# Six-layer local-attention network: scaling on POOL, values through a copy by DMA, feed-forward once per 512 tokens

## What is computed

```python
# DIM 128, DEPTH 6, HEADS 16, DIM_HEAD 64, WINDOW 32, DIM_INNER 341
def attn_layer(x, Wqkv, qs, ksc, Wo):
    q, k, v = jnp.split(x @ Wqkv, 3, -1)            # each 16 heads of 64
    q = l2norm(q) * qs
    k = l2norm(k) * ksc
    q = q * cos * scale + rotate_half(q) * sin * scale
    k = k * cos * inv + rotate_half(k) * sin * inv
    out = local_attention(q, k, v)                  # each query sees itself and 32 keys back
    return out @ Wo
def ffn_layer(x, g, bln, W1, b1, W2, b2):
    xn = (x - mu) / jnp.sqrt(var + 1e-05) * g + bln
    a, gate = jnp.split(xn @ W1 + b1, 2, -1)
    return a * jax.nn.gelu(gate, approximate=False) @ W2 + b2
for i in range(DEPTH):
    x = attn_layer(shift_tokens(x), ...) + x        # shift_tokens moves half of the width by one token
    x = ffn_layer(shift_tokens(x), ...) + x
```

## Time and profile before

| | us |
|---|---|
| median of three runs (5686.42 to 5718.4) | 5706.67 |
| the profiled execution | 5696.51 |
| its span, from the first to the last instruction | 5694.7 |
| busy over the span: PE, DVE, ACT, POOL | 4468.9, 3603.6, 2963.1, 1958.8 |
| the stage of the change: first `mix_out` to the last | 2104.7 to 4858.2 |

### The profile page before, as it was taken

The page is one execution under the profiler, slowest core; times in us unless marked ns, Lnnn a source line. Parts: engine busy times, 40 slices in busy tenths (PEclk is TensorE's granted clock), DMA queues, the critical chain, the costliest instruction groups (busy, mean ns, idle before and its releaser), DMA issues. The chain is left out here.

```text
span 5694.7 us, 89214 instructions
## 1 busy us (share of the span) xinstructions
PE 4468.9 (78%) x28284; PEld 3096.7 (54%) x28284; DVE 3603.6 (63%) x7261; ACT 2963.1 (52%) x8154; POOL 1958.8 (34%) x1203
## 2 busy tenths in 40 slices
PE   6887987888644458888888888888888888588788
PEld 4655665555411136666666666666666666355566
DVE  5554224455578867777777777777777777344422
ACT  3333434443233336666666666666666666233433
POOL 3433003232045444444444444444444434122300
PEclk8888999999755579999999999999999999566799
DMA  0000000000000010000000000000000000000000
GB/s 18 1 2 35 0 0 20 1 1 14 3 0 0 0 50 1 0 0 22 0 0 22 0 0 22 0 0 22 0 0 0 0 0 1 17 1 0 0 30 7
DMA packets 26280, 41.43 MB, mean 7 GB/s; under 512 B 12112, under 2 KB 18664, under 8 KB 25448
## 3 DMA queue, kind: packets, MB, share of 16 engines
q1 hardware_dynamic: 26088, 39.04, 2.0%
HBM read 36.93 MB, written 2.10 MB: 7 GB/s over the span
## 5 line engine op out<-in xcount | busy, mean ns | idle before, releaser
L1426 PE MATMUL ps<-l2f_wqkv,l2f_xsT 128*128 (+3 forms) x1536 | 741.4, 605 | 97.1 <-DVE xnT L1621 90.3
L1358 POOL TENSOR_TENSOR l2f_rn<-l2f_ss,neghalf 128x16 f32<-128x16 f32 x192 | 564.7, 2941 | 436.1 <-DVE l2f_ss L1615 436.1
L1803 ACT ACTIVATE l2f_p<-ps,l2f_negmax 128x96 f32<-128x96 f32 x1536 | 501.7, 338 | 282.7 <-DVE l2f_negmax L1646 279.1
L1364 POOL TENSOR_TENSOR l2f_cosd<-xnT,l2f_rot 128x1024 f32<-128x1024 f32 x192 | 487.2, 2542 | 174.8 <-DVE xnT L1621 174.8
L1484 PE MATMUL ps<-l2f_pT,l2f_vw 96*128 96x128 f32 x3072 | 423.1, 281 | 40.4 <-DVE l2f_pT L1668 40.4
L1426 PEld LDWEIGHTS ps<-l2f_wqkv,l2f_xsT 128*128 128x128 f32 (+1 forms) x1536 | 243.4, 178 | 347.8 <-issue 197.4
L1818 ACT COPY l2f_oT<-ps 64x256 f32<-64x256 f32 x768 | 281.3, 366 | 269.8 <-PE ps L1484 258.3
L1484 PEld LDWEIGHTS ps<-l2f_pT,l2f_vw 96*128 96x128 f32 x3072 | 381.7, 195 | 61.4 <-issue 56.5
L1384 POOL TENSOR_TENSOR l2f_rstd<-l2f_mv,neghalf 128x1 f32<-128x1 f32 x96 | 52.8, 550 | 1051.5 <-DVE l2f_mv L1680 1051.5
L1457 PEld LDWEIGHTS ps<-l2f_kT,l2f_qz 128*128 128x128 f32 x3072 | 399.2, 194 | 1.4 <-issue 0.3
L1457 PE MATMUL ps<-l2f_kT,l2f_qz 128*128 128x96 f32 x3072 | 398.7, 273 | 0.0
(11 more groups left out here) (354 smaller groups left out, 10607.0 us busy)
## 6 DMA issues: line engine op xcount, KB each, us to landing
l2f_wqkv<-L_ffn_Wqkv_dram SPq DMA_DIRECT2D x18, 512.0 KB
l0f_w<-L_w_dram SPq DMA_DIRECT2D x2, 2304.0 KB
l3f_w<-L_w_dram SPq DMA_DIRECT2D x2, 2048.0 KB
l2f_wo<-L_ffn_Wo_dram SPq DMA_DIRECT2D x6, 512.0 KB
l2f_w<-L_ffn_W_dram SPq DMA_DIRECT2D x6, 341.0 KB
l2f_b<-L_ffn_b_dram SPq DMA_DIRECT2D x6, 341.0 KB
l1f_w<-L_w_dram SPq DMA_DIRECT2D x1, 1152.0 KB
k_turn<-l3a_kF SPq DMA_DIRECT2D x4, 256.0 KB, 2.0
```

Source lines behind the costliest of these rows:

```text
L1358: nc.gpsimd.tensor_tensor(rn[:, k], ss[:, k], g.neghalf[:, 0:HEADS], ALU.pow).then_inc(rn_ready, 1)
L1364: nc.gpsimd.tensor_tensor(cosd[:, k].rearrange("p (h d) -> p h d", d=DH), nrm[:, k].rearrange("p (h d) -> p h d", d=DH), rot[:, k, 0, t].u ...
L1426: ins = nc.tensor.matmul(g.ps[0:rows, 2 * (k % 2) + hf], x, wqkv[:, bass.ds(weight_slot(it), 1), c0 + hf * 512:c0 + (hf + 1) * 512] .rearr ...
L1803: ins = nc.scalar.activation(p[:, n % 2, c], g.ps[:, 4, c * KW:(c + 1) * KW], ACT.Exp, bias=negmax[:, col:col + 1], accum_out=rowsum[:, co ...
```

## The change

- **Scaling**: `scale` moves from DVE to POOL. DVE keeps the reciprocal (`inverse_sums`), and POOL's slot takes the four products between its other work.
- **Values**: they are projected once for 128 tokens (k = 2 only, in banks 0 and 1), copied by ACT into `vt`, and moved by two or three DMAs of SP into the two windows of `vw`. `copy_values` stands ahead of the last `exps`. `turn_qk(ahead, 0)` moves on PE ahead of `turn(now, 3)`, and `copy_q` on ACT ahead of `copy_outputs(now, 2)`.
- **Feed-forward**: it runs once in an iteration, one iteration late (`fed`), in the slots t = 1 (three matmuls of 128 x 512 for the gates, their copies, one GELU over 128 x 1536), t = 2 (three matmuls for the other half, product on DVE with the bias) and t = 3 (twelve matmuls with W2, `feed_out` over 512 tokens). Hidden units lie on partitions, so the transposes and their copies go. POOL copies W1 and its biases (`fix_weights`) once in an iteration.
- The loop of the program has two iterations in its body; at the end three slots of feed-forward alone are added. SP loads the first layer's weights after `band_ready`, and the next ones behind the values of a layer's first iteration.

The diff, cut to the queues and the new functions:

```diff
+            final = Iteration(ITERATIONS - 1, 1)
+            for stages in slots(final, last=True):
                 slot(*stages)
-            slot(NONE, NONE, (ITERATIONS - 1, TILES - 1))
+            slot(NONE, NONE, (final, TILES - 1), NONE)
+            for t in range(1, TILES):
+                slot(NONE, NONE, NONE, (final, t))
...
+            def move_values(it, t):
+                w = QBS * (t % 2)
+                sp.wait_ge(v_copied, at(it, TILES, t + 1))
+                sp.wait_ge(pv_done, at(it, STEPS2, PER * (t - 1)))
+                if t:
+                    sp.dma_start(vw[0:WINDOW, w], vt[P - WINDOW:P, (t - 1) % 2]).then_inc(v_moved[t % 2], 16)
+                sp.dma_start(vw[WINDOW:KW, w], vt[0:QB, t % 2]).then_inc(v_moved[t % 2], 16)
+                sp.dma_start(vw[:, w + 1], vt[P - KW:P, t % 2]).then_inc(v_moved[t % 2], 16)
+            sp.wait_ge(band_ready, 1)
+            load_weights(0)
+            for it in range(ITERATIONS):
+                for t in range(TILES):
+                    move_values(it, t)
+                if it % BATCH == 0 and it // BATCH + 1 < DEPTH:
+                    load_weights(it // BATCH + 1)
...
+            def scale(it, t, i):
+                if t is None:
+                    return
+                n = PER * t + i
+                if t == 3 and i == 3:
+                    pool.wait_ge(hT_ready, at(it, 3, -3))
+                pool.wait_ge(rinv_ready, at(it, STEPS2, n + 1))
+                nc.gpsimd.tensor_tensor(
+                    p[:, n % 2], p[:, n % 2],
+                    rinv[:, QUAD * n:QUAD * (n + 1)].unsqueeze(2).broadcast_to([P, QUAD, KW]), ALU.mult).then_inc(scaled, 1)
+            def fix_weights(it, t):
+                if t == 3:
+                    nc.gpsimd.tensor_copy(w1c[:, it.odd], w1[:, bass.ds(weight_slot(it), 1)]
+                                          .rearrange("p a c -> p (a c)")).then_inc(w1_ready, 1)
+            def slot(ahead, now, behind, fed):
                 inverse_deviation(*behind)
+                scale(*now, 0)
                 inverse_norms(*ahead, 0)
+                scale(*now, 1)
+                inverse_norms(*ahead, 1)
                 scaled_rotary(*ahead)
-                inverse_norms(*ahead, 1)
                 cosines(*ahead, 0)
+                scale(*now, 2)
                 cosines(*ahead, 1)
+                scale(*now, 3)
+                fix_weights(*now)
...
-                if k < 2:
-                    x, rows, c0 = xsT[:, WINDOW + t * P:WINDOW + (t + 1) * P], P, k * HD
-                else:
-                    w = QBS * t + k - 2
-                    x, rows, c0 = xsT[:, w * QB:w * QB + KW], KW, 2 * HD
+                    pe.wait_ge(nrm_ready, at(it, 2 * TILES, 2 * t + 1))
+                x, c0 = xsT[:, WINDOW + t * P:WINDOW + (t + 1) * P], k * HD
...
+            def hidden(f, t, c):
+                if t not in (1, 2):
+                    return
+                pe.wait_ge(w1_ready, at(f, 1, 1))
+                pe.wait_ge(xnT2_ready, turned_behind(f, t))
+                if t == 2 and not c:
+                    pe.wait_ge(hg_ready, at(f, 3, 3))
+                if c:
+                    pe.wait_ge((hg_ready, hT_ready)[t - 1], at(f, 3, c))
+                r0, rows = CH[c]
+                c0 = (DI, 0)[t - 1] + r0
+                nc.tensor.matmul(g.ps[0:rows, 7], w1c[:, f.odd, c0:c0 + rows], xnT2[:, f.odd],
                                  start=True, stop=True).then_inc(hid_ready, 1)
...
+            def feed(f, t):
+                if t != 3:
+                    return
+                pe.wait_ge(xnT2_ready, turned_behind(f, t))
+                pe.wait_ge(hT_ready, at(f, 3, 3))
+                for n in range(TILES):
+                    for c, (r0, rows) in enumerate(CH):
+                        ins = nc.tensor.matmul(g.ps[:, 7, n * P:(n + 1) * P], hT[0:rows, c, n * P:(n + 1) * P],
+                                               w2[0:rows, bass.ds(weight_slot(f), 1), c].rearrange("p a c -> p (a c)"),
+                                               start=(c == 0), stop=(c == 2))
                 ins.then_inc(ff_ready, 1)
-            def slot(ahead, now, behind):
+            def slot(ahead, now, behind, fed):
                 mix(*behind)
                 turn_y(*ahead)
                 scores(*now, 0)
@@ -1559,19 +1635,18 @@
                 scores(*now, 2)
                 turn(*now, 1)
                 pv(*now, 0)
-                hidden(*behind, 1)
+                hidden(*fed, 0)
                 scores(*now, 3)
                 project(*ahead, 2)
                 turn(*now, 2)
                 pv(*now, 1)
-                hidden(*behind, 0)
-                project(*ahead, 3)
+                hidden(*fed, 1)
+                turn_qk(*ahead, 0)
                 turn(*now, 3)
                 pv(*now, 2)
-                turn_hidden(*behind)
-                turn_qk(*ahead, 0)
+                hidden(*fed, 2)
+                feed(*fed)
                 pv(*now, 3)
-                feed(*behind)
                 turn_qk(*ahead, 1)
...
-            def scale(it, t, i):
+            def inverse_sums(it, t, i):
                 if t is None:
                     return
                 n = PER * t + i
                 dve.wait_ge(probs_ready, at(it, STEPS2, n + 1))
                 nc.vector.reciprocal(rinv[:, QUAD * n:QUAD * (n + 1)],
                                      rowsum[:, QUAD * n:QUAD * (n + 1)]).then_inc(rinv_ready, 1)
-                dve.wait_ge(rinv_ready, at(it, STEPS2, n + 1))
-                nc.vector.tensor_tensor(
-                    p[:, n % 2], p[:, n % 2],
-                    rinv[:, QUAD * n:QUAD * (n + 1)].unsqueeze(2).broadcast_to([P, QUAD, KW]), ALU.mult).then_inc(scaled, 1)
...
+            def gate_hidden(f, t, c):
+                if t != 2:
+                    return
+                rows = CH[c][1]
+                dve.wait_ge(hid_ready, at(f, 6, 4 + c))
+                dve.wait_ge(gelu_ready, at(f, 1, 1))
+                dve.wait_ge(ff_ready, at(f, 1, 0))
+                nc.vector.scalar_tensor_tensor(hT[0:rows, c], g.ps[0:rows, 7], w1c[0:rows, f.odd, HB + c:HB + c + 1],
+                                               hg[0:rows, c], ALU.add, ALU.mult).then_inc(hT_ready, 1)
+            def feed_out(f, t):
+                if t != 3:
+                    return
+                dve.wait_ge(ff_ready, at(f, 1, 1))
+                nc.vector.tensor_tensor(yt[:], g.ps[:, 7].rearrange("p (t d) -> p t d", d=D), ym[:, f.odd],
+                                        ALU.add).then_inc(yt_ready, 1)
+                dve.wait_ge(yt_ready, at(f, 1, 1))
+                nc.vector.tensor_tensor(g.gate[:, bass.ds((f & (BATCH - 1)) * TILES, TILES), :], yt[:],
+                                        b2[:, bass.ds(weight_slot(f), 1), :].broadcast_to([P, TILES, D]),
                                         ALU.add).then_inc(y_ready, 1)
...
-            def slot(ahead, now, behind):
+                nc.vector.tensor_tensor(ym[:, it.odd, t], yb[:, t], g.ps[:, 6, 0:D], ALU.add).then_inc(y_mixed, 1)
+            def slot(ahead, now, behind, fed):
                 fetch(*ahead)
                 mix_out(*behind)
                 maxima(*now, 0)
                 affine_of(*behind)
                 moments_of(ch, *behind)
-                scale(*now, 0)
+                inverse_sums(*now, 0)
                 normalize_shifted(*behind)
                 maxima(*now, 1)
                 norms(ch, *ahead, 0)
                 copy_probs(*now, 0)
-                scale(*now, 1)
+                inverse_sums(*now, 1)
                 maxima(*now, 2)
                 norms(ch, *ahead, 1)
                 copy_probs(*now, 1)
                 normalize(*ahead, 0)
-                scale(*now, 2)
+                inverse_sums(*now, 2)
                 maxima(*now, 3)
-                bias_hidden(*behind, 1)
                 swap(ch, *ahead, 0)
                 normalize(*ahead, 1)
-                scale(*now, 3)
+                inverse_sums(*now, 3)
                 copy_probs(*now, 2)
-                bias_hidden(*behind, 0)
+                gate_hidden(*fed, 0)
                 rotate(ch, *ahead, 0)
-                gate_hidden(*behind)
+                gate_hidden(*fed, 1)
                 swap(ch, *ahead, 1)
                 copy_probs(*now, 3)
+                gate_hidden(*fed, 2)
+                feed_out(*fed)
                 rotate(ch, *ahead, 1)
-                feed_out(*behind)
...
-            def copy_values(it, t, j):
+            def copy_values(it, t):
                 if t is not None:
-                    act.wait_ge(projected, at(it, 4 * TILES, 4 * t + j + 3))
-                    nc.scalar.copy(vw[:, (QBS * t + j) % (2 * QBS)], banks(2 * j, 2)[0:KW]).then_inc(v_copied, 1)
+                    act.wait_ge(projected, at(it, 3 * TILES, 3 * t + 3))
+                    for u in (t - 2, t - 1):
```

(33 more changed lines are left out.)

158 lines of the change are left out of this document (67 added, 91 removed).

## The result

The changed kernel takes **6439.23 us** (median of 4 runs, 6422.83 to 6443.82) against 5705.01 of the kernel before (4 runs beside it). The ratio is 1.128, with an interval from 1.125 to 1.132. The prediction said 6140, with a range from 5850 to 6370: the sign is right, but the loss is 734 us where 443 were expected, and the time lies outside the range.

A forecast was written before the change was run, and what follows sets the result against it. It took a slot to be bound by a chain of handovers between engines, no single engine being full. 5696.5 + 343 (slots) + 15 (start and end) + 86 (clock falls) = 6140 us, range 5850 to 6370.

The forecast's parts named there:

- The second turn: PE's second turn of p in a slot: 2.5 us later, since POOL's second scaling stands behind a power of 2.91 us.
- The price of a scaling: One scaling product on POOL: 0.83 us taken, up to 1.4 with a wait for the port behind one DVE product.
- The fourth maxima: DVE's fourth maxima in a slot: moved from 3045.45 to about 3047.95 by the later second turn, with no slack.
- The copy of the values: Values' part on PE and ACT: saved projection (1.9 us of PE) and second copy lie off the path, DMAs mostly hidden.
- The three copies behind `copy_q`: ACT's third `copy_outputs`, PE's fourth `pv`, ACT's fourth `copy_outputs` follow one after the other behind `copy_q`; `mix` starts 1.9 us later.
- The saved projection: PE's dropped second projection of the values: 1.9 us of PE, said to lie off the path.
- The clock: PE's clock falls after idle waits, in three of four slots: 72 falls at 1.2 us (0.9 to 2), 86 us.
- The rival that the clock stays down: A fall lasts a whole slot, doubling PE's part of the chain: 6370 if in a third of slots, 7000 in all; chance 0.15.
- The slots: Slots t = 0 to 3 of the stage: 30.3, 32.7, 30.5, 36.4 us, sum 129.9 against 115.58; 343 us over 24 iterations.
- The last gates: ACT in slot t = 1: gates 0.6, table 1.28, GELU 1.6 us ahead of the last `copy_outputs`; 1.1 of 3.5 hidden.
- `feed`: PE in slot t = 3: twelve W2 matmuls ahead of the fourth `pv`, 2.7 us.
- Start and end: Kernel's start (weights after `band_ready`) and end (three more slots in a row): some 15 us more.

## Why the prediction was wrong

**The second turn: right.** It was put 10.43 us after the slot's `mix_out` (3042.96 − 3032.53) and lies at 10.22 (3269.65 − 3259.43), waiting 2.35 us for POOL at the end of a power. In the kernel before with POOL scaling, the clock held up gave back only 41 of 383 us, so it is this queue that the scaling loses by.

**The price of a scaling: right where nothing meets it, too low where VectorE does.** Alone it takes 0.83 us. The group's mean is 1.205; the whole range, from the query of that line:

```profile
L1447 POOL TENSOR_TENSOR l2f_p<-l2f_p,l2f_rinv x384: 822/827/3533, 2097.2 to 5571.2; 128x384 f32<-128x384 f32 x192
```

The first two of a slot are always near 0.83, the fourth takes 2.23 in the mean. The long ones are like this fourth scaling, beside VectorE's products:

```profile
3172.90 3.53 POOL L1447 TENSOR_TENSOR l2f_p<-l2f_p,l2f_rinv 128x384 f32<-128x384 f32 x1 [0.41 <-DVE l2f_rinv L1732]
...
3173.33 1.21 DVE L1716 TENSOR_TENSOR l2f_cosd<-l2f_cosd,xn 128x1024 f32<-128x1024 f32 x1
3174.47 1.28 DVE L1707 TENSOR_TENSOR xn<-xnT,l2f_rot 128x512 f32<-128x512 f32 x2
```

The prediction let POOL lose to one product at most (1.4 us in all); here it ends 0.7 us after the last of VectorE's three products (the second row has two) and pays 2.70 us more than alone. The Trainium skill, "SBUF — State Buffer", Who interferes with whom, has the second requester wait for the whole of the first; the trace agrees with the full block. It adds that POOL can lose to three products in a row, and that the order of the recorded starts does not tell who loses: POOL's row begins 0.43 us ahead of VectorE's first.

**The fourth maxima: nearly right.** Put at 15.42 us, found at 16.22; the 0.8 are the scores at half clock (1.86 for 1.03).

**The copy of the values: the step that failed.** The text said: "The projection saved (1.9 us of PE) and the values' second copy lie off the path." It looked at what the part removes and not at where the copy that stays had moved: ahead of the fourth exponentials on ACT. That put the third projection on the path to the fourth reciprocal, to VectorE's first rotation behind it and to `turn_qk`, which comes at 24.33 us and not at 22.47. Taking this one move back gave 131 us; that run's slot t = 0 has 31.8 us, with `turn_qk` at 22.83 (3223.96 − 3201.13). So, while POOL scales, this move carries 3.4 of the 4.9 us by which t = 0 lies above its forecast. The three copies behind `copy_q` come in the order that was forecast, but not in a row: in the slot shown ACT waits 0.52 and 2.16 us between them for `pv` at half clock.

**What removed work does: the other half of that step.** The saved projection was booked as free; on the kernel before it costs 147 us, all of it by the clock. The products of the hidden layer left PE's wait ahead of the fourth scores empty as well: 2.27 us in the changed kernel where 1.70 stood.

**The clock: too cheap, in the price of a fall and in their count.** Two slots with t = 0 of the same trace show the price. In the one above, the stretch from `turn_qk` on ran at 0.50, and `mix` starts 8.90 us behind `turn_qk` (3292.66 − 3283.76; 5.8 were forecast). In the other, which begins at 4437.53 and takes 33.58 us, that stretch ran at full clock; its windows, and PE's rows:

```profile
4461.50:4465.50 4.00, 2.43 (x20) 2.24 (x20) 3.21 (x6) 2.69 (x4) 0.00 (x0) 1.00 0.25 88
4465.50:4471.10 5.60, 5.49 (x34) 5.48 (x35) 0.00 (x0) 1.81 (x4) 0.00 (x0) 0.70 0.00 0
```

```profile
4461.61 1.10 PE L1515 MATMUL ps<-ident,l2f_cosd 128*128 128x128 f32 x8 [3.35 <-DVE l2f_cosd L1716]
...
4468.15 2.93 PE L1572 MATMUL ps<-l2f_wo,l2f_oT 128*128 x16
```

There `mix` starts 6.54 us behind `turn_qk`. So the fall costs 2.36 us on the path, twice the 1.2 predicted (0.9 to 2). The two whole slots differ by only 1.63 us (35.21 − 33.58), since the other one's clock falls later, at `mix` (0.70; 2.93 us for 1.95). And 72 falls were counted for the stage, where the rows show 76 slow third projections and 64 slots with a slow `turn_qk`: one to two falls in a slot, the first of them on the path because of the copy's place. The products without a use put the clock at some 200 us, for 86 in the sum. The rival that the clock stays down (6370) was the nearest to the time, though not in its mechanism: the clock comes back in every slot, as the forecast said (of the first projections of the 96 slots 2 are slow), and falls again.

**The slots.** 30.3, 32.7, 30.5 and 36.4 were forecast, and without the loop they are 35.18, 35.73, 33.23 and 39.23: over by 4.9, 3.0, 2.7 and 2.8, in sum 13.5 an iteration. The forecast's clock held 3.6 of these; the other 9.9 are 238 us in 24 full iterations. What the feed-forward adds to a slot was sized better than the slot itself: t = 3 was put 6.1 above t = 0 and lies 4.1 above. The last gates (0.69), the GELU (1.48 for 1.6) and its table (1.28) came as priced:

```profile
3324.72 1.28 ACT L1911 ACT_TABLE_LOAD   x1
3326.02 1.48 ACT L1911 ACTIVATE l2f_hg<-l2f_hg 128x1536 f32<-128x1536 f32 x1
```

So did `feed` (2.84 for 2.7, at full clock) and the two sums behind it (0.69 each). With the copy's place alone taken back, t = 0 and t = 2 come to 31.8 and 31.3 us.

**The loop: a term that was missing.** The diff doubles the loop's body, and no line of the prediction says what that does. 67 us.

**Start and end: too small.** Some 15 us were put down; the traces without the loop and before show 37.

In sum: the 95 slots from the first `mix_out` to the last took 637 us more where 429 were forecast (343 and 86), start and end 22 more than forecast, and the loop 67. These are 297; the prediction missed by 299.

What stays open: how the loss is to be shared out exactly. Scaling costs 383 or 248, the order of `turn_qk` gains 56 or loses 155, and the copy's place loses 131 or 8, by what else is there. The parts meet in one chain of handovers, and a share belongs to an order of undoing, not to a part. That the clock's fall is what the feed-forward's bursts cost beyond their own length is argued from the waits and the half-speed rows behind them; the runs with unused products didn't isolate it, as they raised the clock of the stage by 0.02 at most (0.90 to 0.92, 0.89 to 0.90).

## What to carry to other kernels

In a chain of handovers, cost an edit by what stands in front of each waiting instruction after it, on every engine that it reorders, and above all for the steps that are only moved; the copy that was "off the path" came to lead it. Work taken from PE is a gain only if PE's waits don't grow with it: look at the granted clock of the stretch behind a wait, and test by doing the saved product in vain. An engine that is idle half the time is no free place: its queue is, or is not, free at the moment at which the operand comes.

## What the hardware showed that was not expected

A projection whose output nobody reads made a kernel 147 us faster (5863 to 5716), with the clock at 0.99 in place of 0.89 over 2000 us. A loop body of two iterations in place of one cost 53 us over ten jumps back, with 3.0 to 3.6 us of "issue" on DVE at each, and more than doubled the bytes of an instruction queue (1.64 to 3.85 MB); the changed kernel without a jump showed no such wait in its slots and fetched less code than with the loop (3.24 MB for 3.67). And POOL's product of 0.83 us took 3.53 beside three products of VectorE that came back to back.
